# A twelve-layer transformer kernel on one core: a cross attention's inner order and copies, and another's loads and order

## The reference

```python
def _L2_xattn_ref(x1, x2, x3, mask, Wq, Wk, Wv):
    q = jnp.einsum('bsd,hd->bsh', x1, Wq)
    k = jnp.einsum('bsd,hd->bsh', x2, Wk)
    v = jnp.einsum('bsd,hd->bsh', x3, Wv)
    scores = jnp.einsum('bqh,bkh->bqk', q, k) * scale
    weights = jax.nn.softmax(scores + mask, axis=-1)
    out = jnp.einsum('bqk,bkh->bqh', weights, v)
```

## Time and profile before

| what | value |
|---|---|
| median of 3 runs | 2986.35 us |
| the runs | 2976.28, 2986.35, 2987.12 us |
| the profiled execution's own time | 2974.7 us |
| its span in the profile | 2972.9 us (1.8 us less) |
| granted TensorE clock, mean | 0.956 |
| busy: PE, weight loads, DVE, ACT, GpSimd | 2699.4, 1858.4, 1657.2, 1114.7, 609.4 us |

### The profile page before, as it was taken

The page is one execution under the profiler, slowest core; times in us unless marked ns, Lnnn a source line. Parts: engine busy times, 40 slices in busy tenths (PEclk is TensorE's granted clock), DMA queues, the critical chain, the costliest instruction groups (busy, mean ns, idle before and its releaser), DMA issues. The chain is left out here.

```text
span 2972.9 us, 43154 instructions
## 1 busy us (share of the span) xinstructions
PE 2699.4 (91%) x17159; PEld 1858.4 (63%) x17159; DVE 1657.2 (56%) x3739; ACT 1114.7 (37%) x1993; POOL 609.4 (20%) x316
## 2 busy tenths in 40 slices
PE   5899999999999999689999878998996788889978
PEld 2566666666666666456767645665983367868846
DVE  5656565665656554646666555773551251067755
ACT  2343434344343432215555536641331252311123
POOL 2040403122131400000000004771001051145402
PEclk9999999999999999899999989998998989989989
DMA  4223242332323211231010001115758527653101
GB/s 155 78 72 104 75 117 74 104 96 77 100 70 107 70 48 36 86 112 46 24 45 24 1 6 37 43 36 191 259 223 277 163 79 287 226 178 133 67 14 35
DMA packets 101277, 295.48 MB, mean 99 GB/s; under 512 B 8728, under 2 KB 59110, under 8 KB 94422
## 3 DMA queue, kind: packets, MB, share of 16 engines
q1 hardware_dynamic: 97078, 283.75, 30.3%
q0 software_dynamic: 2976, 8.13, 0.8%
q10 hardware_dynamic: 1024, 0.86, 0.1%
HBM read 280.64 MB, written 11.54 MB: 98 GB/s over the span
## 5 line engine op out<-in xcount | busy, mean ns | idle before, releaser
L1904 PE MATMUL L_xattn_bank<-L_xattn_keys_tok,L_xattn_probsT 128*128 128x257 f32 x1664 | 426.1, 395 | 10.0 <-ACT L_xattn_probsT L1721 2.9
L1833 PE MATMUL L_xattn_wide<-L_xattn_keys_feat,weights_a 128*128 128x512 f32 (+2 forms) x1024 | 380.9, 515 | 2.5 <-ACT L_xattn_keys_feat L1741 1.2
L1904 PEld LDWEIGHTS L_xattn_bank<-L_xattn_keys_tok,L_xattn_probsT 128*128 128x128 f32 x1664 | 295.4, 189 | 103.8 <-issue 47.3
L1833 PEld LDWEIGHTS L_xattn_wide<-L_xattn_keys_feat,weights_a 128*128 128x128 f32 x1024 | 189.0, 190 | 153.6 <-issue 123.6
L1490 DVE COPY L_xattn_k_normed<-L_xattn_wide 128x833 f32<-128x833 f32 (+1 forms) x128 | 131.1, 1024 | 192.0 <-PE L_xattn_wide L1833 192.0
L2850 DVE TENSOR_TENSOR_SCAN L_attn_state<-L_attn_decay,L_attn_banks 128x1024 f32<-128x1024 f32 x80 | 182.7, 2286 | 70.9 <-PE L_attn_banks L3052 70.9
L1715 ACT ACTIVATE L_xattn_scores<-L_xattn_scores,L_xattn_neg_max 128x897 f32<-128x897 f32 x128 | 126.4, 1035 | 221.9 <-DVE L_xattn_neg_max L1515 221.9
L2956 POOL TENSOR_TENSOR L_attn_state<-L_attn_state,L_attn_C_rows 128x1024 f32<-128x1024 f32 x80 | 188.7, 2360 | 71.5 <-DVE L_attn_state L2850 71.4
L3052 PEld LDWEIGHTS L_attn_banks<-L_attn_B_diagonal,L_attn_dt_u_tok 128*128 128x128 f32 x1280 | 150.9, 194 | 66.1 <-issue 64.5
L1510 DVE CUSTOM_DVE_ANT_0 L_xattn_scores<-L_xattn_wide,L_xattn_mask_row 128x897 f32<-128x897 f32 x128 | 134.9, 1088 | 96.9 <-issue 96.9
L2119 DVE CUSTOM_DVE_ANT_0 L_xattn_scores<-L_xattn_banks,L_xattn_mask 128x512 f32<-128x512 f32 (+1 forms) x256 | 131.4, 570 | 92.5 <-issue 92.5
(11 more groups left out here) (519 smaller groups left out, 4715.0 us busy)
## 6 DMA issues: line engine op xcount, KB each, us to landing
L_xattn_k_scale<-L_xattn_k_scale_rows SPq DMA_DIRECT2D x128, 417.0 KB, 5.0
L_xattn_ctx_feat<-in_ctx_feat SPq DMA_DIRECT2D x24, 1601.0 KB, 10.0
L_ffn_expert_w<-in_x_L_ffn SPq DMA_DIRECT2D x16, 2056.0 KB, 8.5
L_ffn_expert_w<-in_x_L_ffn SPq DMA_DIRECT2D x17, 1024.0 KB, 5.5
L_ffn_expert_w<-in_x_L_ffn SPq DMA_DIRECT2D x15, 1028.0 KB, 5.8
L_xattn_keys_tok<-in_ctx_tok SPq DMA_DIRECT2D x8, 1536.0 KB
L_attn_C_rows<-L_attn_c_rows SPq DMA_DIRECT2D x48, 256.0 KB, 3.2
L_xattn_ctx_tok<-in_ctx_tok SPq DMA_DIRECT2D x8, 1536.0 KB
```

What stands on the lines that cost most here:

```text
L1833: last = nc.tensor.matmul(wide[:, 2 * h + c, 0:n], wk[:, k, p * P:(p + 1) * P], xnT[b % 2][:, k, a:a + n], start=(k == 0), stop=(k == KT - 1))
L1904: last = nc.tensor.matmul(bS[:, 0:D + 1], pT[:, c, a, :, :].rearrange("p h q -> p (h q)"), xn[b % 2][:, t, :], start=(i == 0), stop=(i == ...
```

## The change

L0 cross attention: the third group of turned tiles has three, the fourth four, so ACT copies 4 + 3 tiles and DVE 3 + 4; `MIX_ORDER` follows; the wait for DVE's copy moves from mix tile 4 to mix tile 6. `apply_v` is written as eight matmuls with 32 output partitions, and stands behind `means`. `swap_max` stands behind the last tile of `mix`. The transposes of the norms of the next batch move from group 3 to group 1 (once per batch).

L2 cross attention: features and masks of batches 0 and 1 are loaded by L1's experts, behind the weights of their tile 8, into free columns of `weights_a` (which grows by 63 columns). Tokens come from a new input `ctx_tok_by_row`, made by the host, in which the rows that one partition receives lie in one piece (13 tiles, the last padded); each is loaded in two parts (7 and 6 tiles), with a semaphore for each part. The ring of tokens has four buffers, the ring of scores one; queries and result use buffers of the layer. On PE the scores of pair u+1 stand between the turned weights and the mix of pair u, the turning of the mixed context of pair u-1 before them; `keep_busy` stays for the first pair alone. On DVE, `scores_taken(u + 1)` comes before `divide(u)`.

```diff
-WCOLS = (9478, 3072)
+WCOLS = (9541, 3072)
+def load_l2_ahead(L, sp):
+    for b in range(2):
+        sp.dma_start(L.ctx_ahead[b], L.aps["ctx_feat"][b].rearrange("(k p) n -> p k n", p=P)).then_inc(L.ctx_ahead_loaded, 16)
+    for j in range(2):
+        sp.dma_start(L.mask_ahead[j * S:(j + 1) * S, :], L.aps["mask_BSS2"][j]).then_inc(L.ctx_ahead_loaded, 16)
...
-    RING = 3
+    RING = 4
+    HALVES = [(0, 7), (7, CT)]
...
+                def load_tok(u):
+                    for h, (a, c) in enumerate(HALVES):
+                        for j in range(2):
+                            b = 2 * u + j
+                            if b >= RING:
+                                sp.wait_ge(mixed, (b - RING) // 2 + 1)
+                            sp.dma_start(ck[b % RING][:, a:c, :], L.aps["ctx_tok_by_row"][b, :, a:c, :]
+                                         ).then_inc(ck_loaded[b % RING][h], 16)
...
                 for u in range(1, PAIRS):
...
+                    load_feat(2 * u)
+                    load_feat(2 * u + 1)
+                    load_mask(u)
+                    load_tok(u - 1)
+                load_tok(PAIRS - 1)
                 L.load_next_weights(sp)
...
+                scores(0)
+                keep_busy(L, ps[:, 4, :], 4)
                 for u in range(PAIRS):
-                    scores(u)
-                    keep_busy(L, ps[:, 4, :], 4)
                     turn_weights(u)
+                    if u >= 1:
+                        turn_mixed(u - 1)
+                    if u + 1 < PAIRS:
+                        scores(u + 1)
                     mix(u)
-                    turn_mixed(u)
+                turn_mixed(PAIRS - 1)
...
-    GROUPS = [(0, 0, 4), (0, 4, 3), (1, 0, 4), (1, 4, 3)]
-    MIX_ORDER = [(c, a) for part in (range(4), range(4, HALF_T)) for c in range(2) for a in part
+    GROUPS = [(0, 0, 4), (0, 4, 3), (1, 0, 3), (1, 3, 4)]
+    MIX_ORDER = [(c, a) for part in (range(3), range(3, HALF_T)) for c in range(2) for a in part
...
-                    if tiles[0] == 4:
-                        pe.wait_ge(pT_odd, 2 * s + 2)
...
+                        if i == 6:
+                            pe.wait_ge(pT_odd, 2 * s + 2)
...
-                    for h in range(2):
-                        c = (2 * p + h) * DH
-                        for k in range(KT):
-                            last = nc.tensor.matmul(bO[h * DH:(h + 1) * DH, 256:256 + S], wv[:, k, c:c + DH],
+                    for k in range(KT):
+                        for j in range(4):
+                            c = 2 * p * DH + 32 * j
+                            h = j // 2
+                            last = nc.tensor.matmul(bO[32 * j:32 * (j + 1), 256:256 + S], wv[:, k, c:c + 32],
                                                     ohT[:, k, h * S:(h + 1) * S], start=(k == 0), stop=(k == KT - 1))
...
                         means(s + 1)
+                    if s >= 2:
+                        apply_v(s - 2)
                     if behind:
                         mix(s - 1, range(4, 6))
...
-                    if s >= 2:
-                        apply_v(s - 2)
                     if behind:
-                        mix(s - 1, range(6, 11))
+                        mix(s - 1, range(6, TILES))
                     if s < STEPS:
                         swap_max(s)
-                    if behind:
-                        mix(s - 1, range(11, TILES))
...
+    AHEAD_AT = 8
...
+                    if shared and j == AHEAD_AT:
+                        load_l2_ahead(L, sp)
```

79 lines of the change are left out of this document (38 added, 41 removed).

## The result

The changed kernel takes 2946.33 us (median of 4 runs, 2940.95 to 2950.07) against 2984.39 (4 runs of the kernel before beside it): ratio 0.9877, 95% interval 0.9854 to 0.9899. That is 38 us less. The forecast was 2940 in a range of 2915 to 2968. The profiled execution took 2943.97 us, 30.7 less than the profiled one of before (2974.7), at nearly the same clock (0.955, before 0.956). So the two profiles show 30.7 of the 38 us; the interval of the ratio is 30 to 44 us.

The account below looks back on a forecast made before the run. PE was taken to bound L0 and L1's expert tiles, DMA L2 with PE's chain nearly as long; -22 + 4 - 24 = -42 us from the 2986 median gives 2944, named 2940, range 2915 to 2968.

Parts of the forecast that it names:

- L0, copies: L0 steps, turned tiles split 4/3 and 3/4: ACT's copy ends earlier, gain 0.22 us a step, bounds 0.10 and 0.30.
- L0, values: L0 steps, value matmuls moved behind the means: 0.25 us for 0.39, gain 0.14 a step, bounds -0.39 to 0.22.
- L0, maxima: L0 steps, exchange of maxima behind the mix: under 0.6 us later, head 0 has 2.3 us in hand, costs nothing.
- L0, the cover behind DVE: L0 steps: DVE's copy, up to 0.19 us longer, stays covered, as `keys_normed` ends at 549.32, before the scores at 550.27.
- L0, the sum: L0: 0.22 + 0.14 = 0.36 us a step, times 62 steps, 22 us less.
- L1: +4: L1's expert tiles: loads ahead delay tile 9's tokens 1.9 us and weights 1.7, cost 4 us, bounds 0 and 9.
- L2: -24: L2 cross attention: shorter loads and PE chain, 26 us less, minus 2 for waits, gives 24 less; bounds 26 and 15.5.
- Price by instruction: L0 rival: 16 value instructions priced by number, 28 ns each, 0.45 us; L0 gives 10 us, total -30, 2956; chance 0.15.
- Tokens no faster by row: L2 rival: tokens stay at 341 GB/s, L2 gives 17 us, total -35, 2951; chance 0.12.
- The slower rival: L0: 32-wide value matmuls do not run together, 0.11 us each, +1.37 a step; total +51, 3037; chance 0.04.
- Something else last in L0: L0 rival: DVE or ACT's exponentials take back what the two edits give; total -20, 2966; chance 0.08.
- Loads ahead harm the tiles after: L1 rival: expert tiles 9 to 14 all wait, 9 us instead of 4; total -37, 2949; chance 0.04.

## Why the prediction was right, point by point

- *L0, copies: 0.22 us a step.* Right. Alone it makes the period 16.68 for 16.90, and the mix begins at 0.31 (forecast 0.30).
- *L0, values: 0.25 us for the group, gain 0.14.* The gain was right (16.68 to 16.52, 0.16), its make-up was not, so that its size is in part luck: the group takes 0.33 to 0.34, the top of my bound of 16 x 21 ns, and the means ahead of it give back 0.11, which I had only as a sentence on the Trainium skill's rule. The reason that I gave for the price, that the four groups of columns run together, is refuted for these products: in turn they cost 0.03 us more.
- *L0, maxima: costs nothing.* Right in the steps with keys, where L1906 is followed by 3 us of keys. The step that failed is the count of steps: two of the 64 have none behind the exchange, and there the exponentials are waited for 1 us longer each, with some more at half clock behind it. And I had not seen that leaving it in place would have cost 0.34 a step, nor that its new place is what lets DVE come last in p=2.
- *L0, the cover behind DVE.* This is the other step that failed. I took `keys_normed` as the last thing that the scores wait for and counted 1 us of margin; behind it stands `key_clamp`, 0.59 us, for which they wait too, and the margin came from an ordinary step. In the step with three blocks of statistics nothing was left: 0.45 us in each of 7 batches, 3.1 us. ACT has a step of its own like this: in p=7 PE waits for its copy of the next key features, and the step gained 0.17 instead of 0.38, by an estimate 0.2 us in each of 7 batches, 1.5 us.
- *L0, the sum.* From the second exchange to the 63rd, 61 periods, it is 1017.1 us for 1036.4, -19.3 where 61 x 0.36 is 22.0; without the stall it is 22.4. The ends give back 6.4: 2.3 up to the first exchange, 0.7 in the first period, 2.3 in the last and 1.1 after it. The first of these is no effect of the change (the exchange comes at 95.3 to 97.6 us in kernels of equal code up to there).
- *L1: +4.* 5.6. I had two waits, 1.9 for tokens and 1.7 for weights; there was one, 4.06 for tokens, and 1.6 at half clock behind it. That none came later was right. The mis-sized term is the end of the loads ahead. Counted from the issue of tile 8's second weights, PE wanted the tokens 18.0 us later (forecast 17.9) and the loads ahead were to end 19.4 us later; the last mask landed 21.9 us later (2149.08 - 2127.22), the tokens 0.2 behind it. The features moved as forecast (413 to 420 GB/s from 2134 to 2140). What was missing is the time to landing, which I had counted in L2 and not here: in the trace's list of packets the last of the loads ahead starts at 2147.5 and lands 1.5 us later. And while the masks moved (228 GB/s from 2142 to 2146) and after, 73 packets of tile 9's first weights, 1.2 MB, which had been issued 4.4 us behind the tokens, moved as well. Whether they held the masks or the tokens up no run shows.
- *L2: -24.* -20.3 between the two profiles, -22.8 against the mean of the three unchanged L2 (101.7). From the stage's first filler to the end of the last mix the forecast was 73.7 us and 2 for waits; it is 2305.70 + 5.83 - 2232.15 = 79.4: 2.1 more in the first projection, at half clock, 4.7 for waits (2.26 and 0.70, and 1.7 in the mix behind), 1.1 less in turning. The mis-sized term is the waits: 2 us in the forecast, 4.7 measured. The rate of the tokens, 422, came out at 419.
- *The total.* 2946 for 2940 is closer than the parts were: the forecast has -42 in the three stages, the two profiles -27.6 (-12.9 + 5.6 - 20.3). The rest of the measured 38 is the scan of L1, 3.1, which is no effect of the change, and 7.4 between the medians' difference and the profiles'. That the total came within 6 us is partly luck; that it is inside the range is not.
- *Rivals.* Price by instruction: 32-wide instructions of 64 and of 128 columns both take 21 ns, so their columns do not set the price; but eight 64-wide ones take 0.39 us, 49 ns each, so their number alone does not either. Tokens no faster by row: refuted. The slower rival, from 59 ns an instruction: refuted. Something else last in L0: true twice a batch, for 3.1 us (DVE) and some 1.5 (ACT), and in the last two steps, not for 22. Loads ahead harm the tiles after: refuted, one wait alone.
